# Splitting the output scales of the last three chunks between POOL and VectorE in a fused attention and expert kernel

## The chip, the cores and the metric

The kernel runs on one core of a Trainium2 chip. The metric is the time of one execution on the device in microseconds (us), the median of several runs. A profiled execution gives the trace from which the rows below are taken; its span is the time from the first to the last instruction that the profile shows.

## The reference

The input `x` is 2 x 512 tokens of 256 features, all in float32. It is normalised over its features to `xn`, and two blocks read `xn`; the result is `x + attention(xn) + experts(xn)`.

- Attention has 16 heads of 16 features: `q`, `k`, `v` and a gate from four 256x256 weights, scores `q k^T` times a decay `gamma^(i-j)` for j <= i (no softmax), `y = scores v`. Then `y` is normalised over its 256 features, `(y - mean) * rsqrt(var + 1e-5) * ln_w + ln_b`, multiplied by `silu(xn wg^T)` and projected by `wo`.
- The expert block routes each token to 4 of 32 experts (softmax over the 4 best router values, times 1.8). An expert is `silu(x gate^T) * (x up^T)` with 192 hidden features, then a projection back to 256. A shared expert of the same shape is added for every token.

The change concerns the factor `rsqrt(var + eps)` of the normalisation of `y`, here called the output scale, and `-mean * rsqrt(var + eps)`, here called the shift.

## The kernel before

The 1024 tokens are cut in 8 chunks of 128, numbered 0 to 7 and called turns where the loop over them is meant (the constant NT is 8, the constant CPB, chunks in a sequence, is 4). Each engine runs its own instructions in the order in which they were written; nothing is reordered, and the engines meet at semaphores only. An instruction that waits holds up all that is behind it on its engine.

The attention runs as one loop over the chunks, with the stages of neighbouring chunks interleaved by hand. In parallel the tokens are routed, and lists (codes) of the tokens of each expert are made. Then come the expert steps 0 to 16. A step handles a pair of experts, its units 2s and 2s+1 being the two experts: TensorE transposes gathered token rows, multiplies them by the gate and up weights (line 1575), ScalarE applies silu (lines 640, 641), VectorE multiplies (lines 1160, 1162), TensorE projects down (lines 1589, 1591), VectorE copies the result (line 1168) and POOL scatters it. The tail of the attention, that is the outputs of chunks 5, 6 and 7, is woven into expert steps 0 to 2. At the end come the shared expert and the weighted sum of the scattered rows.

The output of chunk t goes round the engines in this way:

1. TensorE ends `y` of the chunk (line 1515), ScalarE copies it (line 613), TensorE transposes it (line 1524), ScalarE copies it again (line 617, `ytok`).
2. VectorE takes mean and variance (`output_moments`, lines 1150 to 1153), and signals `mo_sb`.
3. POOL computes the scale (`output_scale`): the power -0.5 of the variance (line 794), one Newton step in two instructions (lines 795, 796), and the shift (line 797), which signals `nm_sb`. Each waits for the one before.
4. ScalarE normalises the chunk with scale and shift (`normalise_output`, line 624).
5. `gate_output` multiplies by `ln_w`, adds `ln_b` and multiplies by the gate. For chunks 2, 5, 6 and 7 that is done by VectorE (lines 1142, 1143, 1145), for the others by POOL (lines 806, 807, 809).
6. TensorE transposes it back (line 1532), ScalarE copies (line 609), TensorE projects (line 1541), VectorE adds the residual (line 1136, `res_sb`).

POOL also issues the gathers of token rows (line 830) and the scatters of results (line 838). Each of these is an indirect DMA; there are 36 of either, one for each block of 128 rows. The order on POOL from turn 6 on is: gathers 0 to 3, the decayed queries of chunk 7, gathers 4 and 5, the spread values of chunk 7, the scale of chunk 5, gather 6, the scale of chunk 6, gather 7, the scale of chunk 7, gathers 8 to 11, and then gathers and scatters in turn. TensorE's transposes of gathered rows (line 1553) take gathers 0 and 1 for the first pair, 2 and 3 for the second, 4 and 5 for the third.

The order on VectorE at the end of turn 7 is: the decayed scores of chunk 7, the moments of chunk 6. Then comes expert step 0: the multiplications of unit 0, gating of chunk 5, moments of chunk 7, gating of chunk 6, residual of chunk 5, multiplications of unit 1. In expert step 1: multiplications of unit 2, gating of chunk 7, multiplications of unit 3, residual of chunk 6.

The order on ScalarE there is: silu of unit 0, normalise chunk 5, copy the outputs of chunk 7 (line 613), the tokens of pair 1 (line 630), the output tokens of chunk 7 (line 617), silu of unit 1, the transposed chunk 5 (line 609), normalise chunk 6, the tokens of pair 2, silu of unit 2, the transposed chunk 6, normalise chunk 7.

The order on TensorE there is: transpose of chunk 7's outputs, gate and up of unit 1, transpose back of chunk 5; then expert step 1: transpose the rows of pair 2 (gathers 4 and 5), project chunk 5, gate and up of unit 2, transpose back of chunk 6, gate and up of unit 3, project chunk 6, down of pair 0, transpose back of chunk 7.

Two waits of TensorE belong to this stretch. The transpose back of a chunk writes the half bank from which the residual of the chunk before is read, and the gate and up matmuls of unit n write the bank of unit n - 2:

```python
need(pe, res_sb, t)            # transpose_back(t)
need(pe, h_sb, 2 * (n - 1))    # gate_up(n)
```

Functions and signals beyond these keep their meaning in the change. The functions that it touches, and those that call them:

Of the kernel before, what the change touches and what calls it, by code (L numbers as in the profile page):

```python
# [11 lines left out]
ALU = mybir.AluOpType  # L12
# [6 lines left out]
NT = TOK // P  # L19
# [31 lines left out]
YRING = 4  # L51
T_RANK, T_INVERT, T_EXPERT = 2, 6, 6
POOL_HOT = range(5, 10)
HOT_STEPS = {(3, "y"): 5, (4, "z"): 6, (4, "rows"): 2, (5, "tok"): 1, (5, "qk"): 2, (5, "vg"): 11}
HOT_PARTS = 2

# [89 lines left out]
def build(nc, x, consts, decay, w_router, w_qkvg, w_out, lnwb, rbias, w_exp, w_late, w_ovf2, w_shared, xn_rows, xnt_rows, y_rows, out):  # L146
    with ExitStack() as ctx:
# [3 lines left out]
        def sem(name):  # L151
            return ctx.enter_context(nc.semaphore(name))
# [9 lines left out]
        def early(*shape, dt=F32):  # L162

            n = int(np.prod(shape)) * mybir.dt.size(dt) // 4
            ap = arena[:, used[0]:used[0] + n]
            used[0] += n
            assert used[0] <= arena.shape[1]
            if dt != F32:
                ap = ap.bitcast(dt)
            if len(shape) == 2:  # L170
                ap = ap.rearrange("p (a b) -> p a b", a=shape[0])
            return ap
# [76 lines left out]
        ystats = early(6)  # L249
        yhalf = early(2)  # L250
        ynewton = early(1)
        yvar = early(2)
        minus_half = early(NT)
        ymv = early(2, 2)
        yrstd = early(2)
        shift_y = early(2)
# [81 lines left out]
        ytok_sb = sem("ytok_sb")  # L338
        mo_sb = sem("mo_sb")
        nm_sb = sem("nm_sb")  # L340
        vg_ps = sem("vg_ps")
        vg_sb = sem("vg_sb")
        xnt_out = sem("xnt_out")
# [432 lines left out]
        def _(pool):  # L776
            steps = [0]

            def step(ins):

                steps[0] += 1
                ins.then_inc(pool_seq, 1)
                pool.wait_ge(pool_seq, steps[0])
# [6 lines left out]
            def output_scale(t):  # L790

                s = slice(t % 2, t % 2 + 1)
                pool.wait_ge(mo_sb, t + 1)
                step(nc.gpsimd.tensor_tensor(yrstd[:, s], yvar[:, s], minus_half[:, 0:1], ALU.pow))
                step(nc.gpsimd.tensor_scalar(ynewton[:, :], yrstd[:, s], yrstd[:, s], yhalf[:, s], ALU.mult, ALU.mult))
                step(nc.gpsimd.tensor_scalar(yrstd[:, s], ynewton[:, :], 1.5, yrstd[:, s], ALU.add, ALU.mult))
                nc.gpsimd.tensor_scalar(shift_y[:, s], yrstd[:, s], ymv[:, t % 2, 0:1], -1.0, ALU.mult, ALU.mult
                                        ).then_inc(nm_sb, 1)
# [119 lines left out]
        def _(dve):  # L918
            steps = [0]

            def step(ins):

                steps[0] += 1
                ins.then_inc(dve_step, 1)
                dve.wait_ge(dve_step, steps[0])
# [131 lines left out]
            def one_hot_positions(part):  # L1057
                a = slice(part * NA // HOT_PARTS, (part + 1) * NA // HOT_PARTS)
                dve.wait_ge(abs_sb, a.stop - len(POOL_HOT))
                dve.wait_ge(pool_hot_sb, len(POOL_HOT))  # L1060
                nc.vector.tensor_scalar(pos_hot[:, a, :], pos_hot[:, a, :], 0.0, None, ALU.is_equal).then_inc(pos_hot_sb, 1)
# [72 lines left out]
            def add_residual(t):  # L1134
                dve.wait_ge(o_ps, t + 1)
                nc.vector.tensor_tensor(x_sb[:, t, :], x_sb[:, t, :], ps_po[:, D:2 * D], ALU.add).then_inc(res_sb, 1)

            def gate_output(t):
                dve.wait_ge(yn_sb, t + 1)
                if t in (CPB - 2, NT - 3):  # L1140
                    dve.wait_ge(z_sb, t)
                step(nc.vector.tensor_tensor(z1[:, :], yn[:, t % 2, :], lnw[:, :], ALU.mult))
                step(nc.vector.tensor_tensor(z1[:, :], z1[:, :], lnb[:, :], ALU.add))
                dve.wait_ge(vg_sb, 2 * (t + 1))
                nc.vector.tensor_tensor(z[:, t % 2, :], z1[:, :], gate[:, t % 3, :], ALU.mult).then_inc(z_sb, 1)

            def output_moments(t):
# [4 lines left out]
                nc.vector.tensor_scalar(yvar[:, t % 2:t % 2 + 1], ymv[:, t % 2, 1:2], EPS, None, ALU.add)  # L1152
                nc.vector.tensor_scalar(yhalf[:, t % 2:t % 2 + 1], ymv[:, t % 2, 1:2], EPS, -0.5, ALU.add, ALU.mult).then_inc(mo_sb, 1)

            def multiply_unit(n):

                dve.wait_ge(sil_sb, 2 * (n + 1))
                gu, p, c = ps_gu[n % 2], n // 2, slice(2 * P, 3 * P)
                need(dve, dn_ps, 2 * (p - 1))
                nc.vector.tensor_tensor(hA[:, n % 4, :], silA[:, n % 2, :], gu[:, P:2 * P], ALU.mult).then_inc(h_sb, 1)  # L1160
                half = slice(0, I2) if n % 2 == 0 else slice(I2, P)
                nc.vector.tensor_tensor(hC[half, p % 2, :], silC[0:I2, n % 2, :], gu[0:I2, c], ALU.mult).then_inc(h_sb, 1)
# [21 lines left out]
            def expert_step(s):  # L1184
                if s < PAIRS:
                    multiply_unit(2 * s)
                if s == 0:
                    gate_output(NT - 3)
                    output_moments(NT - 1)
                    gate_output(NT - 2)  # L1190
                    add_residual(NT - 3)
                if s == 1:
                    gate_output(NT - 1)
                if s == 2:
                    add_residual(NT - 1)
                    nc.vector.memset(o_mem.rearrange("p (j n) -> p j n", j=SUBS)[0:I2, :, XW:OW], 0.0).then_inc(oz_sb, 1)
                if s == PAIRS - 1:
                    results(s - 1)
                if s < PAIRS:
                    multiply_unit(2 * s + 1)  # L1200
                if s == 1:
                    add_residual(NT - 2)
                if s - 2 in O_BASE:
                    overflow_result(O_BASE.index(s - 2))
                if s - 1 in O_BASE:
                    dve.wait_ge(osil_sb, 2 * (O_BASE.index(s - 1) + 1))
                    multiply_overflow(oh_sb)
                if 1 <= s and s != PAIRS - 1:
                    results(s - 1)

            for t in range(NT):
                for r in range(HG // 2):
                    if t == NT - 1 and r == 2:
                        update_state(t - 1)
                    if t == T_INVERT and r == 3:
                        take_inverse()
                        make_codes()
                        find_block_experts()
                    decay_scores(t, r)
                    if t == 0 and r == 0:  # L1220
                        refine(2, slice(2, NT))
                        for u in range(2, 6):
                            normalise(u)
                if t == 0:
                    normalise(6)
                    normalise(7)
                if t == T_RANK - 1:
                    take_logits()
                if t % CPB > 0 and t < NT - 1:
                    update_state(t - 1)  # L1230
                if t == 0:
                    decay_keys(t)
                if t == T_RANK - 1:
                    choose_experts()
                if t == T_RANK:
                    mark_choices()
                if t == T_RANK + 1:
                    choose_slots()
                    assign_slots()
                if t == T_RANK + 2:  # L1240
                    gate_output(CPB - 2)
                    dve.wait_ge(pos_sb, 1)
                    one_hot_blocks()
                    add_residual(t - 2)
                if t >= 1:
                    output_moments(t - 1)
                if t == T_RANK - 1:
                    choices_as_numbers()
                if t == T_RANK:
                    take_ranks()  # L1250
                    count_blocks()
                if t == T_RANK + 3:
                    code_blocks(1)
                    one_hot_positions(0)
                if t == T_EXPERT:
                    weigh_choices()
                if 2 <= t < NT - 1 and t != T_RANK + 2:
                    add_residual(t - 2)
                if t == T_RANK:
                    shift_ranks()  # L1260
                if 0 < t % CPB < CPB - 1 or t == CPB:
                    decay_keys(t)
                if t == T_RANK + 2:
                    code_blocks(0)
                if t == T_RANK - 1:
                    spread_choices()
                if t == T_RANK + 3:
                    one_hot_positions(1)

            for s in range(PAIRS + 1):  # L1270
                expert_step(s)
# [630 lines left out]
```

## Time and profile before

| what | value |
|---|---|
| median of 3 runs | 200.17 us (200.09 to 200.4) |
| the profiled execution's own time | 200.26 us |
| its span | 198.4 us |
| TensorE's granted clock | full in every slice |
| turn 7 and expert step 0 on VectorE | about 76 to 87 us |

An engine's busy time is the sum of the times of its instructions. The chain of waits goes back from the last instruction to what released it, again and again, so that its pieces fill the span. In the timelines a row is an instruction or several alike ones; the bracket at its end says how long the engine was idle in front of it and which instruction of which engine, by line, released it. PEld is TensorE's loading of weights, which goes ahead of a matmul. Names such as `w_mem` cover many small tiles, so the line says what an instruction is.

### The profile page before, as it was taken

What the parts mean: (1) busy time and instruction counts of PE and PEld (TensorE: products, weight loads), DVE (VectorE), ACT (ScalarE), POOL (GpSimd) and SP (SyncE); (2) the same over time, 40 slices, a digit from 0 to 9 for tenths busy, and PEclk for the clock granted to TensorE, in tenths of its full rate; (3) what the DMA queues carried; (4) which work ended last, traced back from release to release, by engine and by line L of the source; (5) the groups of instructions that cost most, each with busy time, mean ns of one, the idle gap of its engine ahead of it and who ended that gap; (6) DMA issues with size and microseconds to landing.
All of it is one profiled execution on the core that took longest, in us unless ns stands there. A gap on an engine that the chain in (4) does not pass through costs nothing.

```text
span 198.4 us, 4872 instructions
## 1 busy us (share of the span) xinstructions
PE 190.0 (96%) x1734; PEld 142.7 (72%) x1734; DVE 117.5 (59%) x360; ACT 96.7 (49%) x242; POOL 111.8 (56%) x156
## 2 busy tenths in 40 slices
PE   8998999999998899899999999999999999999994
PEld 2665756778565667698888678887867877687863
DVE  3478789898897766765632532433342144426894
ACT  3146248555889342653238647734934941123500
POOL 4133057525979468777777677777877743730000
PEclk9999999999999999999999999999999999999999
DMA  4994999998000029999975634324433335229963
GB/s 133 316 374 159 332 403 421 446 444 378 7 0 3 5 56 380 384 358 366 366 288 149 223 106 140 97 90 138 123 104 98 115 91 220 79 82 292 373 262 132
DMA packets 15000, 42.33 MB, mean 213 GB/s; under 512 B 2677, under 2 KB 6138, under 8 KB 14336
## 3 DMA queue, kind: packets, MB, share of 16 engines
q1 hardware_dynamic: 11376, 33.03, 45.5%
q0 software_dynamic: 3456, 8.92, 13.3%
q8 instruction: 14, 0.23, 0.5%
q10 hardware_dynamic: 144, 0.07, 0.2%
q14 instruction: 10, 0.08, 0.1%
HBM read 34.66 MB, written 7.86 MB: 214 GB/s over the span
## 4 chain that ended last, share of the span: by engine, by line
PE 73%; DMA 7%; DVE 7%; issue 4%; POOL 4%; ACT 3%; SPq 0%; ACTq 0%; POOLq 0%; DVEq 0%
PE bank L1575 20%; PE bank L1591 8%; PE bank L1783 5%; PE bank L1589 5%; DMA xg_mem<-xn_rows,codes 4%; PE bank L1440 4%; PE bank L1450 3%; PE bank L1553 3%; DMA w_mem<-w_qkvg_dram 3%; PE bank L1541 3%; PE bank L1612 3%; PE bank L1515 3%; DVE w_mem L1105 2%; PE bank L1465 2%; PE bank L1817 2%
## 5 line engine op out<-in xcount | busy, mean ns | idle before, releaser
L1575 PE MATMUL bank<-xb_mem,w_mem 128*128 128x128 f32 x384 | 47.7, 276 | 0.1
L1575 PEld LDWEIGHTS bank<-xb_mem,w_mem 128*128 128x128 f32 x384 | 45.4, 192 | 0.8 <-issue 0.3
L838 POOL DMA_INDIRECT y_rows<-y_mem,codes x36 | 36.2, 1007 | 16.8 <-issue 9.4
L830 POOL DMA_INDIRECT xg_mem<-xn_rows,codes x36 | 35.4, 984 | 13.0 <-issue 9.7
L1160 DVE TENSOR_TENSOR h_mem<-h_mem,bank 128x128 f32<-128x128 f32 x32 | 9.2, 287 | 42.2 <-ACT h_mem L641 41.9
L1105 DVE TENSOR_TENSOR w_mem<-bank,w_mem 128x512 f32<-128x512 f32 x32 | 20.1, 682 | 2.9 <-PE bank L1465 2.8
L640 ACT ACTIVATE h_mem<-bank 128x128 f32<-128x128 f32 x32 | 8.9, 277 | 23.5 <-PE bank L1575 23.1
L1168 DVE COPY y_mem<-bank 128x256 f32<-128x256 f32 x36 | 15.0, 424 | 7.3 <-PE bank L1591 4.5
L653 ACT COPY w_mem<-w_mem 128x1024 f32 x16 | 16.0, 1042 | 3.2 <-PE bank L1630 2.2
L1591 PE MATMUL bank<-w_mem,h_mem 128*128 128x256 f32 x60 | 17.0, 405 | 0.0
L1440 PE MATMUL bank<-w_mem 128*128 128x128 f32 x128 | 15.9, 278 | 0.2 <-DMA w_mem<-w_qkvg_dram 0.2
L1440 PEld LDWEIGHTS bank<-w_mem 128*128 128x128 f32 x128 | 14.9, 192 | 1.1 <-ACT w_mem L566 0.7
L630 ACT COPY xb_mem<-bank 128x512 f32<-128x512 f32 x16 | 9.4, 585 | 12.6 <-PE bank L1553 12.4
L1450 PE MATMUL bank<-w_mem 128*128 128x512 f32 x32 | 15.1, 593 | 0.0
L1591 PEld LDWEIGHTS bank<-w_mem,h_mem 128*128 128x128 f32 x60 | 10.2, 189 | 5.8 <-issue 5.0
L574 ACT ACTIVATE w_mem<-bank,cst 128x256 f32<-128x256 f32 x16 | 6.7, 470 | 10.0 <-PE bank L1440 10.0
L1783 PE MATMUL bank<-xg_mem,ws_mem 128*128 128x256 f32 x48 | 11.0, 381 | 0.0
L1589 PE MATMUL bank<-w_mem,h_mem 64*128 64x256 f32 x60 | 10.5, 428 | 0.0
L1553 PE MATMUL bank<-cst,xg_mem 128*128 128x128 f32 x64 | 9.7, 275 | 0.7 <-DMA xg_mem<-xn_rows,codes 0.7
L1783 PEld LDWEIGHTS bank<-xg_mem,ws_mem 128*128 128x128 f32 x48 | 9.0, 190 | 1.5 <-DVE h_mem L1292 0.3
L787 POOL TENSOR_TENSOR w_mem<-w_mem,cst 128x256 f32<-128x256 f32 x6 | 5.3, 881 | 8.5 <-ACT w_mem L576 8.5
L1553 PEld LDWEIGHTS bank<-cst,xg_mem 128*128 128x128 f32 x64 | 7.7, 141 | 2.6 <-DMA xg_mem<-xn_rows,codes 0.9
(168 smaller groups left out, 320.7 us busy)
## 6 DMA issues: line engine op xcount, KB each, us to landing
w_mem<-w_exp_dram SPq DMA_DIRECT2D x3, 3456.0 KB, 21.6
w_mem<-w_late_dram SPq DMA_DIRECT2D x7, 1152.0 KB, 8.1
w_mem<-y_rows SPq DMA_DIRECT2D x8, 512.0 KB, 7.3
w_mem<-w_qkvg_dram SPq DMA_DIRECT2D x2, 512.0 KB, 6.3
w_mem<-decay_dram SPq DMA_DIRECT2D x2, 512.0 KB, 7.6
xn_rows<-w_mem SPq DMA_DIRECT2D x2, 512.0 KB, 3.4
xnt_rows<-w_mem SPq DMA_DIRECT2D x1, 1024.0 KB, 4.9
w_mem<-w_ovf_dram SPq DMA_DIRECT2D x16, 64.0 KB
```

The source lines that it names most:

```text
L653: return nc.scalar.copy(o_mem[:, j * OW:j * OW + XW], w_mem[:, bass.ds(e * EW, XW)])
L830: nc.gpsimd.indirect_dma_start(xg[:, k % RING, :], None, xn_rows, bass.IndirectOffsetOnAxis(ap=codes[:, c, 0:1], axis=0),).then_inc(tok_in ...
L838: nc.gpsimd.indirect_dma_start(y_rows, bass.IndirectOffsetOnAxis(ap=codes[:, c, 1:2], axis=0), ysb[:, k % YRING, :], None, bounds_check=RO ...
L1105: nc.vector.tensor_tensor(st[:, 4 * r * P:4 * (r + 1) * P], ps_s[r][:, :], dec[:, 4 * r * P:4 * (r + 1) * P], ALU.mult).then_inc(sc_sb, 1)
L1168: nc.vector.tensor_copy(ysb[:, w, :], ps[:, 0:D]).then_inc(ys_sb, 1)
L1440: last = nc.tensor.matmul(ps_qk[:, m * P:(m + 1) * P], wqkvg[:, g, m * P:(m + 1) * P], tokens(g, t), start=(g == 0), stop=(g == KT - 1))
L1450: last = nc.tensor.matmul(ps_vg[:, :], tokens(g, t), wqkvg[:, g, 2 * D:4 * D], start=(g == 0), stop=(g == KT - 1))
L1553: last = nc.tensor.transpose(ps_xt[p % 2][:, (2 * g + j) * P:(2 * g + j + 1) * P], xg[:, k % RING, g * P:(g + 1) * P], ident)
L1575: last = nc.tensor.matmul(ps_gu[j][:, m * P:(m + 1) * P], w[:, o:o + P], xbT[:, p % 2, (2 * g + j) * P:(2 * g + j + 1) * P], start=(g == 0 ...
L1589: nc.tensor.matmul(ps_dn[j][:, 0:D], hC[rows, p % 2, :], w2[rows], start=True, stop=False)
L1591: nc.tensor.matmul(ps_dn[j][:, 0:D], hA[:, 2 * (p % 2) + j, :], w[:, j * EW + KT * MB:j * EW + XW], start=False, stop=True).then_inc(dn_ps, 1)
L1783: last = nc.tensor.matmul(to, ws_mem[:, o:o + P], xnT_back[:, g, n], start=(g == 0), stop=(g == KT - 1))
```

## The change

For chunks 5, 6 and 7 POOL computes only the power (line 794) and signals it with a new semaphore, `root_sb`. The Newton step and the shift are done by VectorE, in a new function `finish_scale`, with the same operands; the shift there signals `nm_sb`. VectorE calls it for chunk 5 at the end of turn 7, behind the moments of chunk 6. In expert step 0 it calls it for chunk 6 behind the multiplications of unit 0, and for chunk 7 behind the gating of chunk 6. Chunks 0 to 4 stay as they are. The new `step` on VectorE is the same as the one there: the instruction signals, and VectorE waits for it before the next.

```diff
--- before.py
+++ after.py
@@ -51,6 +51,7 @@
 YRING = 4
 T_RANK, T_INVERT, T_EXPERT = 2, 6, 6
 POOL_HOT = range(5, 10)
+DVE_SCALES = (5, 6, 7)
 HOT_STEPS = {(3, "y"): 5, (4, "z"): 6, (4, "rows"): 2, (5, "tok"): 1, (5, "qk"): 2, (5, "vg"): 11}
 HOT_PARTS = 2
 
@@ -249,6 +250,7 @@
         ystats = early(6)
         yhalf = early(2)
         ynewton = early(1)
+        vnewton = early(1)
         yvar = early(2)
         minus_half = early(NT)
         ymv = early(2, 2)
@@ -338,6 +340,7 @@
         ytok_sb = sem("ytok_sb")
         mo_sb = sem("mo_sb")
         nm_sb = sem("nm_sb")
+        root_sb = sem("root_sb")
         vg_ps = sem("vg_ps")
         vg_sb = sem("vg_sb")
         xnt_out = sem("xnt_out")
@@ -791,6 +794,9 @@
 
                 s = slice(t % 2, t % 2 + 1)
                 pool.wait_ge(mo_sb, t + 1)
+                if t in DVE_SCALES:
+                    nc.gpsimd.tensor_tensor(yrstd[:, s], yvar[:, s], minus_half[:, 0:1], ALU.pow).then_inc(root_sb, 1)
+                    return
                 step(nc.gpsimd.tensor_tensor(yrstd[:, s], yvar[:, s], minus_half[:, 0:1], ALU.pow))
                 step(nc.gpsimd.tensor_scalar(ynewton[:, :], yrstd[:, s], yrstd[:, s], yhalf[:, s], ALU.mult, ALU.mult))
                 step(nc.gpsimd.tensor_scalar(yrstd[:, s], ynewton[:, :], 1.5, yrstd[:, s], ALU.add, ALU.mult))
@@ -1152,6 +1158,15 @@
                 nc.vector.tensor_scalar(yvar[:, t % 2:t % 2 + 1], ymv[:, t % 2, 1:2], EPS, None, ALU.add)
                 nc.vector.tensor_scalar(yhalf[:, t % 2:t % 2 + 1], ymv[:, t % 2, 1:2], EPS, -0.5, ALU.add, ALU.mult).then_inc(mo_sb, 1)
 
+            def finish_scale(t):
+
+                c = slice(t % 2, t % 2 + 1)
+                dve.wait_ge(root_sb, t - DVE_SCALES[0] + 1)
+                step(nc.vector.tensor_scalar(vnewton[:, :], yrstd[:, c], yrstd[:, c], yhalf[:, c], ALU.mult, ALU.mult))
+                step(nc.vector.tensor_scalar(yrstd[:, c], vnewton[:, :], 1.5, yrstd[:, c], ALU.add, ALU.mult))
+                nc.vector.tensor_scalar(shift_y[:, c], yrstd[:, c], ymv[:, t % 2, 0:1], -1.0, ALU.mult, ALU.mult
+                                        ).then_inc(nm_sb, 1)
+
             def multiply_unit(n):
 
                 dve.wait_ge(sil_sb, 2 * (n + 1))
@@ -1185,9 +1200,11 @@
                 if s < PAIRS:
                     multiply_unit(2 * s)
                 if s == 0:
+                    finish_scale(NT - 2)
                     gate_output(NT - 3)
                     output_moments(NT - 1)
                     gate_output(NT - 2)
+                    finish_scale(NT - 1)
                     add_residual(NT - 3)
                 if s == 1:
                     gate_output(NT - 1)
@@ -1266,6 +1283,8 @@
                     spread_choices()
                 if t == T_RANK + 3:
                     one_hot_positions(1)
+                if t == NT - 1:
+                    finish_scale(NT - 3)
 
             for s in range(PAIRS + 1):
                 expert_step(s)
```

## Rows read from the trace of the kernel before

**Rows 1.** The page, part 1: busy us of each engine, share of the span, instructions

```profile
PE 190.0 (96%) x1734; PEld 142.7 (72%) x1734; DVE 117.5 (59%) x360; ACT 96.7 (49%) x242; POOL 111.8 (56%) x156
```

**Rows 2.** The chain of waits, expert step 1: start us, us, what

```profile
87.46 1.52 PE bank L1575 x12
```

**Rows 3.** TensorE's waits, 75 to 198 us: us in total, times, longest

```profile
PE bank L1553 <- DMA xg_mem<-xn_rows,codes: 0.7, 1, 0.7
PE bank L1804 <- DVE h_mem L1295: 0.3, 1, 0.3
PE bank L1603 <- DVE h_mem L1162: 0.2, 1, 0.2
PE bank L1524 <- ACT w_mem L613: 0.2, 1, 0.2
```

**Rows 4.** Timeline of VectorE, turn 7 and step 0: start us, us, line, [idle before]

```profile
80.37 0.14 DVE L1153 TENSOR_SCALAR w_mem<-w_mem 128x1 f32<-128x1 f32 x1
80.43 0.28 DVE L1160 TENSOR_TENSOR h_mem<-h_mem,bank 128x128 f32<-128x128 f32 x1
...
81.31 0.42 DVE L1142 TENSOR_TENSOR w_mem<-w_mem 128x256 f32<-128x256 f32 x1 [0.42 <-ACT w_mem L624]
...
85.05 0.42 DVE L1142 TENSOR_TENSOR w_mem<-w_mem 128x256 f32<-128x256 f32 x1 [1.54 <-ACT w_mem L624]
...
86.00 0.43 DVE L1145 TENSOR_TENSOR w_mem<-w_mem 128x256 f32<-128x256 f32 x1
86.34 0.41 DVE L1136 TENSOR_TENSOR x_sb<-x_sb,bank 128x256 f32<-128x256 f32 x1
...
86.98 0.28 DVE L1162 TENSOR_TENSOR h_mem<-h_mem,bank 64x128 f32<-64x128 f32 x1
```

**Rows 5.** Timeline of POOL, scales of chunks 5 to 7 and gathers

```profile
78.89 0.58 POOL L794 TENSOR_TENSOR w_mem<-w_mem 128x1 f32<-128x1 f32 x1
...
80.39 0.26 POOL L797 TENSOR_SCALAR w_mem<-w_mem 128x1 f32<-128x1 f32 x1
81.09 1.06 POOL L830 DMA_INDIRECT xg_mem<-xn_rows,codes  x1 [0.44 <-issue]
...
87.81 1.05 POOL L830 DMA_INDIRECT xg_mem<-xn_rows,codes  x1 [0.44 <-issue]
```

**Rows 6.** Timeline of ScalarE in the same stretch

```profile
80.68 0.60 ACT L624 ACTIVATE w_mem<-w_mem 128x256 f32<-128x256 f32 x1 [0.74 <-POOL w_mem L797]
81.30 0.37 ACT L613 COPY w_mem<-bank 128x256 f32<-128x256 f32 x1
...
83.84 0.27 ACT L641 ACTIVATE h_mem<-bank 64x128 f32<-64x128 f32 x1
...
84.41 0.60 ACT L624 ACTIVATE w_mem<-w_mem 128x256 f32<-128x256 f32 x1
```

**Rows 7.** Timeline of TensorE's weight loads in the same stretch

```profile
81.73 0.20 PEld L1524 LDWEIGHTS bank<-cst,w_mem 128*128 128x128 f32 x2 [0.46 <-ACT w_mem L613]
...
83.23 0.25 PEld L1532 LDWEIGHTS bank<-cst,w_mem 128*128 128x128 f32 x2
84.38 0.42 PEld L1553 LDWEIGHTS bank<-cst,xg_mem 128*128 128x128 f32 x4 [0.89 <-DMA xg_mem<-xn_rows,codes]
...
86.97 0.25 PEld L1532 LDWEIGHTS bank<-cst,w_mem 128*128 128x128 f32 x2
87.38 1.42 PEld L1575 LDWEIGHTS bank<-xb_mem,w_mem 128*128 128x128 f32 x12 [0.16 <-issue]
```

**Rows 8.** Timeline of VectorE: short instructions that wait for one another

```profile
5.13 0.16 DVE L932 TENSOR_TENSOR w_mem<-w_mem 128x1 f32<-128x1 f32 x1
5.33 0.16 DVE L933 SCALAR_TENSOR_TENSOR w_mem<-w_mem 128x1 f32<-128x1 f32 x1
...
68.29 0.25 DVE L1082 TENSOR_SCALAR w_mem<-w_mem,cst 128x60 f32<-128x60 f32 x1
68.58 0.22 DVE L1084 SCALAR_TENSOR_TENSOR w_mem<-w_mem 128x60 f32<-128x60 f32 x1
```

## The prediction

> **What bounds the kernel now.** I read the page's busy shares first [rows 1]: TensorE is busy for 96% of the span, VectorE for 59%, POOL for 56%. So work taken from POOL is worth something only where TensorE waits for it, directly or through others. The chain of waits comes second: from 84.41 us to the end of the expert steps it is TensorE's own matmuls, piece touching piece, and the gate/up matmuls of unit 3, the place that will matter, are one of the pieces [rows 2]. A delay there is a delay of the end, unless a later wait takes it up. Third, whom TensorE waits for after 75 us: 0.7 us once for gathered rows, and 0.2 to 0.3 us three times for ScalarE or VectorE [rows 3]. Then I read the place of the change engine by engine, in the timelines of VectorE, POOL, ScalarE and TensorE's weight loads, which show when TensorE may go on [rows 4 to 7].
>
> What the reader should see there is a ring of in-order engines. VectorE ends the moments of chunk 6 at 80.51 (80.37 + 0.14); the next instruction, which does not wait for them, starts at 80.43, 0.06 behind the start of their last [rows 4]. POOL has long computed the power of chunk 5 (78.89 to 79.47) and delivers its shift at 80.65 [rows 5]. ScalarE, idle for 0.74 us for just that, normalises chunk 5 at 80.68, and only then copies chunk 7's outputs at 81.30 [rows 6]; TensorE's transpose of these waits 0.46 us for the copy and loads at 81.73 [rows 7]. So the scale of chunk 5 is already on TensorE's path, through ScalarE's order.
>
> **The change, part by part.** *POOL.* For each of chunks 5, 6 and 7 three instructions go; for chunk 5 the stretch from the end of the power to the end of the shift is 80.65 − 79.47 = 1.18 us [rows 5]. Behind it stand gather 6, the power of chunk 6, gather 7, the power of chunk 7, gathers 8 and on. Gather 6 starts 0.44 us behind the scale as now, at 79.91 instead of 81.09, and the power of chunk 6 ends at about 79.91 + 1.06 + 0.58 = 81.55. The power of chunk 7 must wait for that chunk's moments, which VectorE now ends at 85.05 − 1.54 = 83.51 [rows 4] and will end 0.76 us later (below), at 84.27; with 0.06 for the signal and 0.58 for itself it is done at 84.9, and gather 8 starts at about 85.4 instead of 87.81 [rows 5]. POOL gains 2.4 us on the gathers from 8 on. It is worth nothing to TensorE: its one wait for gathered rows, at 84.38 [rows 7], is for gathers 4 and 5, and both are issued before chunk 5's scale in POOL's order.
>
> *One finish on VectorE.* Three 128x1 instructions, each waiting for the one before. No row shows a 128x1 with two scalars from memory. The nearest is the refinement at the start, also 128x1 and each waiting for the one before: starts 0.20 us apart, 0.16 us long [rows 8]. The upper bound is a 128x60 with one scalar from memory, 0.25 us long and 0.29 from its start to that of the instruction that waits for it [rows 8]; the lower is a 128x1 that is 0.14 long and holds up the next, which does not wait for it, by 0.06 [rows 4]. I take 0.20. Then the shift is there 2 × 0.20 + 0.16 = 0.56 us after the start, and whatever stands behind is put off by 2 × 0.20 + 0.06 = 0.46 us (bounds 0.18 and 0.64).
>
> The Trainium skill has a lower price (VectorE: DVE Perf Modes, section The TRN2 errata — SBUF-src ops pay a fixed extra latency per instruction): 58 cycles plus the row length at 0.96 GHz for an instruction from SBUF to SBUF, from which I estimate 0.06 us for each of the three. The page itself says that its row is too low for one instruction alone, and the refinement's 0.16 us bear that out [rows 8]; by the rule the sum below would come down to about 0.2 us.
>
> *Chunk 5.* Its finish stands behind chunk 6's moments, so it starts at 80.43, though the power has been there since 79.47. The shift comes at 80.99, and ScalarE starts 0.03 later, as now, at 81.02 instead of 80.68: +0.34 us. Everything behind it on ScalarE is tied to it: the copy of chunk 7's outputs 81.30 → 81.64, TensorE's transpose 81.73 → 82.07 and the gate/up of unit 1 behind it, the gate of unit 1 (83.84 → 84.18), the normalising of chunk 6 (84.41 → 84.75) [rows 6, 7]. TensorE itself gets the 0.34 us back, since at 84.38 it has stood idle for 0.89 us for the gathers [rows 7]; ScalarE does not. If the gathers landed earlier this cover would go, at 0.34 us, but the delay below is longer and takes it in.
>
> *Chunk 6.* Its finish stands behind unit 0's multiplications, which end 0.46 us later than now, and waits for the power at 81.55, so it runs from about 81.61; VectorE's gating of chunk 5 starts at 82.07 instead of 81.31, +0.76 [rows 4]. This third of the change is hidden: a gating takes 86.00 + 0.43 − 85.05 = 1.38 us [rows 4], so chunk 5's ends at 83.45, and TensorE's transpose back of chunk 5 wants it at 83.23 + 0.34 = 83.57 [rows 7]. Were it later, the idle time in front of 84.38 would pay. The shift of chunk 6, at 82.2, is not awaited: ScalarE reaches chunk 6 at 84.75.
>
> *Chunk 7, where it costs.* VectorE's gating of chunk 6 follows ScalarE, 85.05 → 85.39 [rows 4]. Behind it now stands chunk 7's finish (its power is there at 84.9), 0.46 us, and behind that the residual of chunk 5 and the multiplications of unit 1. Both are 0.34 + 0.46 = 0.80 us late. Two waits of TensorE hang on them. The transpose back of chunk 6 needs the residual of chunk 5, since both use one bank: 86.34 + 0.41 + 0.80 = 87.55, plus 0.06 for the signal (as from ScalarE's end at 81.67 to the load at 81.73 [rows 6, 7]), 87.61 instead of 86.97: 0.64 us. The gate/up matmuls of unit 3 need unit 1 multiplied, since they write its bank: 86.98 + 0.28 + 0.80 + 0.06 = 88.12 instead of 87.38 [rows 4, 7]. Together TensorE is 88.12 − 87.38 = 0.74 us late; in the trace of before the same chain leaves it 0.06 us to spare. Chunk 7's shift comes at 87.3, ahead of ScalarE's need of it.
>
> *Behind that.* ScalarE and VectorE follow TensorE, and of its waits there none is for something that keeps its own time: two rows remain, both for VectorE's multiplications that follow TensorE's own matmuls [rows 3]. So nothing gives the 0.74 us back. Sum: 0.34 + 0.46 − 0.06 = 0.74 us. With the lower price the shift comes at 80.43 + 0.12 + 0.14 = 80.69, +0.04, and the sum is 0.04 + 0.18 − 0.06 = 0.16; with the upper at 80.43 + 0.58 + 0.25 = 81.26, +0.61, and it is 0.61 + 0.64 − 0.06 = 1.19. The profiled execution took 200.26 us, 1.86 of it outside the span; 201.00 it would be. It lies 0.09 above the median of the runs, 200.17, so I forecast 200.91 us, with 200.33 and 201.36 for the bounds.
>
> **The rivals.** *Cheap finishes.* The small instructions run at the pace of those that do not wait, 0.06 us [rows 4]: 200.33 us, no change that can be told. For it: most of a short instruction's time is overlapped on this engine. Against: each of the three waits for the last, as in the refinement [rows 8]. *POOL's lead pays.* Gathers 6 to 11 are issued 1.2 to 2.4 us earlier; if that shortened what TensorE waits for, and the finishes fell into VectorE's idle time, the wait of 0.7 us [rows 3] would be the gain: about 199.5 us, faster. It decides from the point at which gathers 4 and 5 land before TensorE is there (84.38 − 0.89 = 83.49). For it: VectorE stands idle 1.54 us ahead of chunk 6's gating [rows 4]. Against: gathers 4 and 5 are ahead of the removed work, and chunk 7's finish stands behind that idle time, not in it. *More than the sum.* Scalars from memory cost more than any row shows, or the power of chunk 6 comes so late that chunk 5's gating holds TensorE beyond the gathers: from 201.4 us to about 201.7 (a finish of 0.8 us in both terms). *Not doing what it says:* chunk 7's power waits for moments that are themselves later, so POOL's lead may be smaller than 2.4 us; as nobody waits for it, the time would be the forecast's, and it has no chance of its own.
>
> **How the numbers follow.** A measurement of this kernel can tell about 0.2%, 0.4 us, from no change. The forecast's own band, 200.6 to 201.4 us, gets 0.65; cheap finishes, or a delay partly taken up, 200.0 to 200.6, get 0.17; POOL's lead 0.08; more than the sum 0.10. The band and the last are slower by over 0.2%, 0.75; the second is no change, the third faster. The range, 200.3 to 201.5, takes in both bounds and leaves out POOL's lead, part of the second case and most of the worst.
>
> **What would show it.** Right: ScalarE's wait ahead of chunk 5's normalising grows from 0.74 to about 1.1 us and is for VectorE; the finish's instructions start about 0.20 us apart; TensorE's transpose back of chunk 6 and its gate/up of unit 3 wait for VectorE, together 0.74 us; the stretch from there to the end is as long as before; gather 8 starts near 85.4. Wrong: unit 3 starting less than 0.3 us later than 87.38; a later wait of TensorE that has become shorter; or scalars from memory that do not keep the refinement's pace.

## Result and the profile after

The changed kernel takes 203.69 us (median of 6 runs, 203.01 to 204.39), the kernel before, run beside it, 200.25 us: the ratio is 1.0161, 95% interval 1.0129 to 1.0192. It is slower, as forecast, but by 3.4 us and not by 0.7, and outside the range.

The profiled execution after took 203.01 us, span 201.2 us. Line numbers are 3 to 19 higher than before. TensorE's waits after 75 us, and the timelines of VectorE, ScalarE, TensorE's weight loads and POOL follow, in the order of [rows 3], [rows 4], [rows 6], [rows 7] and [rows 5]; their columns are the same.

```profile
PE bank L1543 <- ACT w_mem L616: 0.8, 1, 0.8
PE bank L1551 <- DVE x_sb L1142: 0.5, 1, 0.5
...
PE bank L1560 <- ACT w_mem L612: 0.3, 1, 0.3
```

```profile
81.82 0.14 DVE L1159 TENSOR_SCALAR w_mem<-w_mem 128x1 f32<-128x1 f32 x1
81.88 0.27 DVE L1165 TENSOR_SCALAR w_mem<-w_mem 128x1 f32<-128x1 f32 x1
82.18 0.21 DVE L1166 TENSOR_SCALAR w_mem<-w_mem 128x1 f32<-128x1 f32 x1
82.43 0.21 DVE L1167 TENSOR_SCALAR w_mem<-w_mem 128x1 f32<-128x1 f32 x1
82.56 0.28 DVE L1175 TENSOR_TENSOR h_mem<-h_mem,bank 128x128 f32<-128x128 f32 x1
...
83.63 0.41 DVE L1148 TENSOR_TENSOR w_mem<-w_mem 128x256 f32<-128x256 f32 x1
...
88.31 0.27 DVE L1165 TENSOR_SCALAR w_mem<-w_mem 128x1 f32<-128x1 f32 x1
...
88.99 0.41 DVE L1142 TENSOR_TENSOR x_sb<-x_sb,bank 128x256 f32<-128x256 f32 x1
...
89.62 0.28 DVE L1177 TENSOR_TENSOR h_mem<-h_mem,bank 64x128 f32<-64x128 f32 x1
```

```profile
82.68 0.60 ACT L627 ACTIVATE w_mem<-w_mem 128x256 f32<-128x256 f32 x1 [1.28 <-DVE w_mem L1167]
```

```profile
83.72 0.20 PEld L1543 LDWEIGHTS bank<-cst,w_mem 128*128 128x128 f32 x2 [1.00 <-ACT w_mem L616]
...
85.59 0.42 PEld L1572 LDWEIGHTS bank<-cst,xg_mem 128*128 128x128 f32 x4
86.56 0.73 PEld L1560 LDWEIGHTS bank<-w_mem 128*128 128x128 f32 x4 [0.56 <-ACT w_mem L612]
...
90.02 1.08 PEld L1594 LDWEIGHTS bank<-xb_mem,w_mem 128*128 128x128 f32 x9 [0.31 <-issue]
```

```profile
80.34 0.57 POOL L798 TENSOR_TENSOR w_mem<-w_mem 128x1 f32<-128x1 f32 x1
...
85.86 0.56 POOL L798 TENSOR_TENSOR w_mem<-w_mem 128x1 f32<-128x1 f32 x1 [1.96 <-DVE w_mem L1159]
86.59 1.00 POOL L836 DMA_INDIRECT xg_mem<-xn_rows,codes  x1 [0.18 <-issue]
```

The gate and up matmuls of unit 3 load at 90.02 us instead of 87.38 [rows 7]: 2.64 us late. Behind them next to nothing is lost: from there to the end of the span it is 201.2 − 90.0 = 111.2 us, before 198.4 − 87.4 = 111.0. The reader should now ask how much of the 2.64 us was there before the first moved instruction ran, and compare an instruction that the change doesn't touch: the last instruction of chunk 6's moments, which ends a run without waits, starts at 81.82 instead of 80.37 [rows 4], 1.45 us late. VectorE is already 1.46 us late at 76.88 us, where the same instruction started at 75.42 before. So only 2.64 − 1.46 = 1.18 us arise where the prediction looked.

The 1.46 us come together earlier: 0.21 us before 58.5 us, the rest at 60 us. These are the rows of before there, POOL's, VectorE's, and TensorE's wait:

```profile
58.51 0.64 POOL L806 TENSOR_TENSOR w_mem<-w_mem 128x256 f32<-128x256 f32 x1 [0.25 <-ACT w_mem L624]
59.22 0.64 POOL L807 TENSOR_TENSOR w_mem<-w_mem 128x256 f32<-128x256 f32 x1
59.94 0.64 POOL L809 TENSOR_TENSOR w_mem<-w_mem 128x256 f32<-128x256 f32 x1
```

```profile
60.09 1.50 DVE L1070 TENSOR_TENSOR h_mem<-xb_mem,cst 128x960 bf16<-128x960 bf16 x1
```

```profile
PE bank L1532 <- POOL w_mem L809: 0.8, 1, 0.8
```

And the same after:

```profile
58.72 0.73 POOL L812 TENSOR_TENSOR w_mem<-w_mem 128x256 f32<-128x256 f32 x1 [0.25 <-ACT w_mem L627]
59.53 0.72 POOL L813 TENSOR_TENSOR w_mem<-w_mem 128x256 f32<-128x256 f32 x1
60.33 1.69 POOL L815 TENSOR_TENSOR w_mem<-w_mem 128x256 f32<-128x256 f32 x1
```

```profile
60.30 1.15 DVE L1076 TENSOR_TENSOR h_mem<-xb_mem,cst 128x960 bf16<-128x960 bf16 x1
```

```profile
PE bank L1551 <- POOL w_mem L815: 2.0, 1, 2.0
```

POOL's gating of chunk 3 is the same code on the same data, but each product takes 0.73 us instead of 0.64. So the third starts at 60.33, 0.03 behind VectorE's product of two inputs in SBUF, where before it started 0.15 ahead of that. Whichever of the two starts second is stretched: before VectorE's took 1.50 us instead of 1.15, after POOL's took 1.69 instead of 0.73. And POOL's is on the path: TensorE's transpose back of chunk 3 waits for it, 0.8 us before and 2.0 after.

The Trainium skill describes this (SBUF — State Buffer, section SBUF: two separate sides): VectorE and GpSimd share a pair of ports as an exclusive lock, also for a VectorE instruction with two SBUF inputs against a GpSimd instruction that reads SBUF, and the one that starts second is blocked. The rows above agree as to who is blocked: 60.30 + 1.15 = 61.45 us is when VectorE's ends, and POOL's ends 0.57 behind that. That is less than the 0.73 us which POOL's product takes alone; what it did ahead of the block no row shows.

### The profile page after: what moved, and what is told of

The parts are those of the page before. It is cut to its first block, busy times and chain, and to the rows that moved or that the text cites. A ratio compares the mean times of both kernels' runs of the same rounds, so it can differ in the third digit from the quotient of the medians.

```text
span 201.2 us, 4872 instructions
## 1 busy us (share of the span) xinstructions
PE 190.1 (95%) x1734; PEld 142.7 (71%) x1734; DVE 118.9 (59%) x369; ACT 96.8 (48%) x242; POOL 110.2 (55%) x147
## 4 chain that ended last, share of the span: by engine, by line
PE 75%; DVE 10%; ACT 4%; DMA 3%; POOL 3%; issue 2%; SPq 1%; ACTq 0%; POOLq 0%; DVEq 0%
PE bank L1594 20%; PE bank L1610 8%; PE bank L1802 5%; PE bank L1608 5%; PE bank L1469 4%; PE bank L1459 4%; DVE w_mem L1111 3%; DMA w_mem<-w_qkvg_dram 3%; PE bank L1534 3%; PE bank L1560 3%; PE bank L1631 3%; PE bank L1572 3%; PE bank L1484 3%; PE bank L1836 2%; ACT xg_mem L594 2%
## 5 line engine op out<-in xcount | busy, mean ns | idle before, releaser
L1334 DVE SCALAR_TENSOR_TENSOR x_sb<-w_mem,rw,x_sb 128x256 f32<-128x256 f32 x22 | 9.5, 477 | 0.2
L1534 PE MATMUL bank<-w_mem 128*32 128x128 f32 x256 | 8.7, 275 | 0.7 <-ACT w_mem L569 0.7
```

## Experiments

Theory A has two causes. First, the diff adds a one-word tile, `vnewton`, in front of some of the tiles that POOL's gating reads and writes (`yn`, `z1`, `z`); it moves these by 4 bytes, POOL's products get slower, and the third loses the race with VectorE. Second, the moved steps cost TensorE 1.18 us, a finish holding VectorE for 0.68 us. The chief rival, B, puts the whole loss on the moved steps. Each kernel ran beside the kernel before on its chip (median 200.53 us for the first group, 200.52 for the second, 200.37 for the third).

**The whole change, the tile laid behind all others** (first group):

```diff
-        vnewton = early(1)          # after ynewton
         zT = early(KT * P)
+        vnewton = early(1)
```

> The change as it is, but the one-word tile of the new Newton step is laid behind all the other tiles of its region, so that no other tile moves by a word. Theory A (the one word moves the tiles behind it; POOL's gating instructions then take 0.73 us instead of 0.64, and the third of chunk 3 starts just behind a VectorE instruction with two inputs in SBUF and is held by it for 1.06 us; the moved steps themselves cost 1.2 us): POOL's gating back at 0.64 us, TensorE's wait for POOL near 60 us back from 2.0 to 0.8, time about 201.4 us. Theory B (the moved steps alone make all of the 3.4 us, and what differs ahead of 76 us is chance): 203.4 to 203.9.

201.73 us, ratio 1.0058 (1.0040 to 1.0076). POOL's products take 0.64 us again and TensorE's wait at 60 us is 0.8. The waits after 75 us are those of the change, 0.8, 0.5 and 0.3, and unit 3 is 1.19 us late, counted from a stretch that begins 0.07 later. By the medians the moved steps are worth 1.20 us; B falls.

**The kernel before with one unused word at that place** (first group):

```diff
         ynewton = early(1)
+        unused_word = early(1)
```

> The kernel before with one unused word in the place where the change lays its new tile; nothing else. Theory A: POOL's gating at 0.73 us, TensorE's wait near 60 us 2.0 us long, time 200.25 + 1.3 to 2.2 = 201.5 to 202.4 (the upper end if TensorE's granted clock dips as in most runs of the change). Theory B: 200.2, as before.

202.61 us, 1.0104 (1.0075 to 1.0133), with every instruction as before. In the profile's groups of instructions (busy us, mean ns) POOL's three products, and TensorE's wait:

```profile
L810 POOL TENSOR_TENSOR w_mem<-w_mem 128x256 f32<-128x256 f32 x4 | 3.9, 971 | 0.3
L807 POOL TENSOR_TENSOR w_mem<-w_mem 128x256 f32<-128x256 f32 x4 | 3.2, 793 | 4.6 <-ACT w_mem L625 4.6
L808 POOL TENSOR_TENSOR w_mem<-w_mem 128x256 f32<-128x256 f32 x4 | 2.9, 728 | 0.3
```

```profile
PE bank L1533 <- POOL w_mem L810: 2.0, 1, 2.0
```

One word costs 2.08 us alone. With the 1.20 us of the moved steps that is 3.28, of the 3.44 measured; the rest is within the intervals.

**The change, with one useless 0.42-us instruction on VectorE ahead of its product** (first group):

```diff
+                nc.vector.bn_stats(...)      # result unused
                 code_blocks(1)
```

> The change as it is, with one more instruction on VectorE (a repeat of the moments' first, 0.42 us, one input) ahead of the 128x960 product that holds POOL near 60 us. Theory A: POOL's third gating instruction of chunk 3 starts first and runs its 0.73 us, VectorE's waits for it; TensorE's wait near 60 us falls to about 0.9 us, time 1.0 to 1.7 us below the change, 202.0 to 202.7, although VectorE has more to do. Rival C (POOL is slow there by itself, for its address or its code): no gain, 203.7 to 204.1.

202.00 us, 1.0068 (1.0054 to 1.0083): 1.5 us above before where the change is 3.4 above it, though VectorE does more. POOL and VectorE at 60 us:

```profile
60.61 0.72 POOL L815 TENSOR_TENSOR w_mem<-w_mem 128x256 f32<-128x256 f32 x1
```

```profile
61.02 1.33 DVE L1076 TENSOR_TENSOR h_mem<-xb_mem,cst 128x960 bf16<-128x960 bf16 x1
```

POOL's third product is first again and takes 0.72 us; the wait is 1.0. So the 0.09 us a product are cheap by themselves, and the order of the two starts is what costs. Rival C, a POOL that is slow there by itself, falls as the cause of the wait.

**Tile at the end, and chunk 7's finish behind the multiplications of unit 1** (first group):

```diff
                     gate_output(NT - 2)
-                    finish_scale(NT - 1)
 ...
                 multiply_unit(2 * s + 1)
+                if s == 0:
+                    finish_scale(NT - 1)
```

> As the first of these, and the finish of chunk 7 stands behind the multiplications of unit 1 instead of in front of the residual of chunk 5. Theory A: 0.6 to 0.7 us less than the first, since only the 0.54 us of chunk 5's shift are left: 200.7 us; TensorE's two waits in expert step 1 fall from 1.2 to 0.5 us. Theory B: no different from the first by more than 0.2 us.

201.31 us, 1.0041 (1.0025 to 1.0057). The wait at the transpose back of chunk 6 is gone, and unit 3 is 0.52 us late instead of 1.19. The trace shows the 0.67 us that were expected, the medians 0.42, and the time stays above the 200.7 expected, by more than the 0.28 that this chip is slower. What remains is chunk 5's finish: the waits for ScalarE (0.8 and 0.4), and with it chunk 6's gating, which VectorE starts at 85.78 instead of 85.05 us in a stretch that begins 0.18 later.

**Chunk 5 back on POOL, chunk 6's finish as in the change, chunk 7's late** (second group; tile at the end, `DVE_SCALES = (6, 7)`):

> The new tile behind all others, chunk 5's scale whole on POOL as before, chunk 6's finish on VectorE where the change has it, chunk 7's behind the multiplications of unit 1. Theory A (of the moved steps only the 0.54 us of chunk 5's later shift and the 0.68 us of chunk 7's finish ahead of unit 1 reach TensorE, and both are gone here; POOL's lead is worth nothing): within 0.3 us of before on the same chip, 0.3 to 0.7 us below the run with chunk 7 late and chunk 5 moved. Rival D (anything moved to VectorE there costs, the third finish too): 0.4 us or more above before.

A miss: 201.79 us, 1.0068 (1.0052 to 1.0084), 1.27 us above before. The number is in rival D's range, but the rows give another reason than a price for anything moved. VectorE, then POOL, then TensorE's wait:

```profile
82.54 0.27 DVE L1165 TENSOR_SCALAR w_mem<-w_mem 128x1 f32<-128x1 f32 x1 [1.91 <-POOL w_mem L798]
...
83.22 0.41 DVE L1148 TENSOR_TENSOR w_mem<-w_mem 128x256 f32<-128x256 f32 x1
```

```profile
81.92 0.58 POOL L798 TENSOR_TENSOR w_mem<-w_mem 128x1 f32<-128x1 f32 x1
```

```profile
PE bank L1550 <- DVE w_mem L1151: 1.4, 1, 1.4
```

With chunk 5's small steps back on POOL, the power of chunk 6 comes at 82.50, and VectorE stands in front of it for 1.91 us with the gating of chunk 5 queued behind. Chunk 6's finish is free in the change only because chunk 5's steps have left POOL. That I had not seen.

**Chunk 5's finish ahead of the moments of chunk 6, chunk 6's behind the gating of chunk 5, chunk 7's late; gathers 4 and 5 ahead of the decayed queries** (second group; tile at the end; of the diff the places of the first two finishes):

```diff
+                if t == NT - 1:
+                    finish_scale(NT - 3)
                 output_moments(...)          # of chunk 6
 ...
-                    finish_scale(NT - 2)
                     gate_output(NT - 3)
+                    finish_scale(NT - 2)
```

> The three finishes on VectorE in other places, and gathers 4 and 5 ahead of the decayed queries of chunk 7 on POOL: chunk 5's finish ahead of chunk 6's moments, chunk 6's behind the gating of chunk 5, chunk 7's behind the multiplications of unit 1; new tile behind all others. Theory A (ScalarE's start on chunk 5 sets TensorE's pace through step 0, with the gathers next in line): the shift of chunk 5 at about 80.4 instead of 80.65, gathers 0.9 us earlier, TensorE at unit 3 about 0.3 to 0.4 us earlier than before: 0.1 to 0.5 us below before on the same chip. Rival D: no faster than before, 0 to 0.8 us above it.

A second miss: 200.74 us, 1.0017 (0.9995 to 1.0038), no difference from before that can be told, where 0.1 to 0.5 us less was expected. ScalarE still waits as long as before:

```profile
80.85 0.60 ACT L627 ACTIVATE w_mem<-w_mem 128x256 f32<-128x256 f32 x1 [0.73 <-DVE w_mem L1168]
```

In this order the finishes cost nothing that can be told, and they gain nothing: chunk 5's shift ends at 80.82 us, not at the 80.4 expected. One reason is in VectorE's rows: its state update, of two SBUF inputs, now runs beside POOL's decayed queries and takes 0.83 us for two instead of 0.58.

**Two and five unused words in the kernel before** (second group):

> The kernel before with two unused words in the place of the new tile. If POOL's time depends on whether the moved tiles lie an odd or an even number of words from the two others that it reads, its gating is back at 0.64 us and the time at before's; if on any other rule of the address (any shift costs), 0.73 us and 1 to 2 us above before.

> The kernel before with five unused words there, so that the moved tiles lie a whole number of 128 bytes from the start of the region. If even words cost, 0.73 us for POOL's gating, TensorE's wait near 60 us 2.0 us, 1 to 2 us above before; if alignment to a larger unit helps, 0.64 us or less and no loss.

202.49 us, 1.0100 (1.0080 to 1.0120), and 201.78 us, 1.0077 (1.0048 to 1.0107). In both POOL's first two products take 0.72 to 0.73 us, the third is blocked, and TensorE waits 2.0. So it isn't a matter of odd and even words.

**Sixteen, eight and four unused words** (third group; four words apart, with one run of each kernel):

> The kernel before with 16 unused words (64 bytes) where the change has its one-word tile; no instruction differs. If the time of POOL's 128x256 products depends on where the tiles lie within a line of 64 bytes: 0.64 us as before, TensorE's wait for POOL at 60 us stays 0.8 us, time as before within 0.3 us. If it depends on anything wider, or on the distance to the tiles that did not move: 0.73 us, the wait 2.0 us, and 1.2 to 2.2 us more.

> The kernel before with 8 unused words (32 bytes) there. If the place within 32 bytes decides: 0.64 us and the time of before within 0.3 us. If the place within 64 bytes decides, and not that within 32: 0.73 us and 1.2 to 2.2 us more, while 16 words cost nothing.

> The kernel before with 4 unused words (16 bytes) in the same place. If POOL's 128x256 products keep their time when the tiles move by 16 bytes: 0.64 us and a wait of TensorE of 0.8 us at 60 us. If only moves by whole multiples of 32 bytes are free: 0.73 us, the wait 2.0 us, and the time 1.2 us or more above the kernel before.

200.57 us, 1.0003 (0.9985 to 1.0021); 200.53 us, 1.0005 (0.9989 to 1.0021); and 200.36 us beside 200.59 for the kernel before. The three products and the wait with four words:

```profile
L810 POOL TENSOR_TENSOR w_mem<-w_mem 128x256 f32<-128x256 f32 x4 | 2.5, 636 | 0.3
L807 POOL TENSOR_TENSOR w_mem<-w_mem 128x256 f32<-128x256 f32 x4 | 2.5, 635 | 3.4 <-ACT w_mem L625 3.4
L808 POOL TENSOR_TENSOR w_mem<-w_mem 128x256 f32<-128x256 f32 x4 | 2.5, 633 | 0.3
```

```profile
PE bank L1533 <- POOL w_mem L810: 0.8, 1, 0.8
```

Moves of 16, 32 and 64 bytes cost nothing, moves of 4, 8 and 20 bytes do: the place within 16 bytes decides; a move of 12 bytes wasn't tried. The Trainium skill names 16 bytes as the line of this memory, each crossing to a new line having its price (SBUF — State Buffer, section Specifications (TRN2)); the unit of the runs agrees with it, but that crossings are the cause isn't shown.

Whether it is the place itself or that in relation to the operands that did not move (`lnw`, `lnb`, the gate) no experiment tells apart, but the allocation in the kernel's text says more. Counted from the start of their region, `lnw`, `lnb` and the gate lie at multiples of 16 bytes. The moved tiles lie 12 bytes past one in the fast kernel before, and at a multiple of 16 in the slow ones with one and five words. So 16-byte alignment is not what makes the product fast. And the decayed queries, a POOL product of the same shape whose first operand and result also lie 12 bytes past a multiple of 16 in that region, take 0.73 us in the kernel before:

```profile
75.25 0.73 POOL L787 TENSOR_TENSOR w_mem<-w_mem,cst 128x256 f32<-128x256 f32 x1
```

The place of these two alone therefore doesn't decide; that of the second operand, here in `cst`, has a part.

**Only chunk 7's finish on VectorE: where the change has it, and behind the multiplications of unit 1** (third group; tile at the end, `DVE_SCALES = (7,)`):

> Chunks 5 and 6 are scaled whole on POOL as before; only chunk 7's finish (two Newton instructions and the shift) is on VectorE, in the place that the change gives it, between the gating of chunk 6 and the residual of chunk 5. The new tile lies behind zT. Theory A (a finish holds VectorE for 0.68 us, as in the trace after, and TensorE's waits at the transpose back of chunk 6 and at unit 3 pass it on, less 0.06 to spare): unit 3's gate/up about 0.6 us later than before, time 0.5 to 0.7 us above the kernel before. Theory F (by the prediction's 0.46 us a finish): 0.3 to 0.4 us above. Rival D (the power without the other instructions on POOL disturbs something else): not within either.

> As the one before, but chunk 7's finish stands behind the multiplications of unit 1, where no wait of TensorE hangs on it. Theory A: the same time as the kernel before within 0.2 us; POOL's two instructions less and its shift less for chunk 7 are worth nothing. Rival (POOL's lead is worth something once VectorE's order costs nothing): 0.3 us or more below the kernel before.

201.05 us, 1.0038 (1.0024 to 1.0051), and 200.67 us, 1.0017 (1.0003 to 1.0032). TensorE's weight loads for unit 3, first in place, then late:

```profile
87.76 1.42 PEld L1591 LDWEIGHTS bank<-xb_mem,w_mem 128*128 128x128 f32 x12 [0.31 <-issue]
```

```profile
87.32 1.41 PEld L1592 LDWEIGHTS bank<-xb_mem,w_mem 128*128 128x128 f32 x12 [0.31 <-issue]
```

Against chunk 6's gating, which starts at 84.75 and 84.99 us (85.05 before), that is 0.68 us late in the first and on time in the second. So one finish in front of the residual costs its full 0.68 us, by the time 0.7, and theory F with 0.46 a finish is out. The late one costs nothing at unit 3; its median lies 0.3 us above before, more than the 0.2 expected. Where that is the traces don't show, and it stays open; the kernel above with all three finishes on VectorE and chunk 7's late is likewise 0.26 us slower by its median (0.78) than by its trace (0.52). In neither is POOL's lead worth anything.

## Why the prediction was wrong

**The step that failed first: the sum begins at 80.43 us.** The part-by-part account takes every row ahead of the first moved instruction as unchanged, and prices what the diff removes, adds and moves among instructions only. The new tile is not in it at all. In the trace it cost 1.46 us at the start of the stretch, and in most runs more (last section); that it is the tile's doing is shown by the kernels with the tile at the end and with the unused word. No rival covers it: *more than the sum* looked at scalars and at the power of chunk 6. In the profile of before there was a sign to be read: POOL's gating stood on the path, 0.15 us from a collision with VectorE.

**The second, a mis-sized term: a finish taken at 0.20 us an instruction.** Its three instructions start 0.30 and 0.25 us apart and last 0.27, 0.21 and 0.21 us: the shift is there 0.76 us after the start (0.56 forecast), and what stands behind is held 0.68 us (0.46). The refinement reads no scalar from memory; here the first instruction reads two (0.27 us), the others one each (0.21). The nearest row in pace was the 128x60 [rows 8], which has one and was taken as the upper bound. With the bound the sum was 1.19 us, and the trace shows 2.64 − 1.46 = 1.18. That the two agree is partly luck, for the terms differ: chunk 5's is 0.54 at its start and 0.51 by the end of chunk 6's gating instead of 0.61, the finish 0.68 instead of 0.64. And the 0.06 to spare isn't there: from the end of unit 1's multiplications to the load for unit 3 it is 0.12 us before (87.26 to 87.38, [rows 4, 7]) and after (89.90 to 90.02), so this wait was at its limit already, and the 0.06 for the signal, taken from ScalarE, was too short for it. The estimate of 0.06 us from the Trainium skill (VectorE: DVE Perf Modes, section The TRN2 errata) is contradicted by the 0.21.

**What was right.** *Chunk 5:* ScalarE's wait is for VectorE and grows from 0.74 to 1.28 us [rows 6], at the forecast place, 0.54 instead of 0.34. *The gathers:* the 0.89 us ahead of pair 2 [rows 7] are gone: TensorE loads these rows 1.21 us later than before and no longer waits for them, while ScalarE gets nothing back. (The cover was a little larger than forecast: the rows landed at least 0.24 us sooner after their issue than in the trace of before, which nothing in the change explains.) One link I missed: projecting chunk 5 now waits 0.3 us for ScalarE's copy; it adds nothing, since unit 3 is held for longer by VectorE. *Chunk 6:* hidden, with the gating of chunk 5 at 83.63 − 1.46 = 82.17 (82.07 forecast); the cover is POOL's lead, as the miss with chunk 5 back on POOL showed. *Chunk 7:* the transpose back of chunk 6 waits 0.5 us for the residual, and unit 3 follows the multiplications; the kernels with only chunk 7 confirm place and price. *POOL's lead:* gather 8 at 86.59 − 1.46 = 85.13 (85.4 forecast, with 0.44 us from the scale to the gather; behind the power alone it is 0.18), POOL idle for 1.96 us ahead of the last power, and nothing gained. *Behind:* the rest is as long as before within 0.2 us.

## What to carry to other kernels

A diff that adds a tile moves every tile behind it: price that as a part of the change, put small new tiles last or fill them up to 16 bytes, so that the others keep their places within 16 bytes, and compare durations of untouched instructions before looking at the touched ones. Where two engines that block each other start 0.15 us apart on the path, a small shift can turn the order (here 0.18 us, two products of 0.09 more each), and the price is close to the length of the instruction that now goes first (here 0.96 us, 1.69 instead of 0.73, behind one of 1.15). A short serial computation handed to another engine costs its full pace, with its own operand forms, in front of whatever is queued behind it; place it behind the work that others wait for.

## What the runs showed of the hardware

*POOL and addresses.* A 128x256 float32 product on POOL takes 0.635 us or 0.73 us by where its tiles lie within 16 bytes, in the kernels with moves of 0, 4, 8, 16, 20, 32 and 64 bytes.

*The clock after an idle time.* In five of the six runs of the changed kernel the granted clock averages 0.992 over the span, in the one profiled here 1.0. The profile with one unused word caught where: windows of 1 us, busy share of PE, PEld, DVE, ACT and POOL (with instructions), then the granted clock.

```profile
60.00:61.00 1.00, 0.01 (x1) 0.00 (x0) 0.97 (x4) 0.92 (x3) 0.92 (x2) 1.00 0.00 0
61.00:62.00 1.00, 0.00 (x0) 0.00 (x0) 1.00 (x2) 0.00 (x0) 1.00 (x2) 1.00 0.06 16
62.00:63.00 1.00, 0.98 (x18) 0.57 (x18) 0.51 (x1) 0.51 (x2) 1.00 (x1) 0.87 0.00 0
63.00:64.00 1.00, 1.00 (x6) 0.80 (x3) 0.00 (x0) 1.00 (x5) 0.90 (x3) 0.50 0.00 0
64.00:65.00 1.00, 1.00 (x3) 0.37 (x2) 0.00 (x0) 1.00 (x5) 0.80 (x5) 0.50 0.00 0
65.00:66.00 1.00, 1.00 (x21) 0.83 (x24) 0.42 (x1) 1.00 (x5) 0.25 (x2) 0.50 0.00 0
66.00:67.00 1.00, 1.00 (x25) 0.63 (x18) 0.00 (x0) 0.86 (x4) 0.00 (x0) 0.92 0.00 0
```

TensorE had done nothing for 2 us and was at work again from 62.02 us; the clock then fell to half, the 1.2 GHz level, and came back after 3 to 4 us. The price is read from TensorE's rows of this kernel (first) and of the one with five words, whose clock stayed full behind the same 2.0-us wait:

```profile
63.11 2.08 PE L1542 MATMUL bank<-w_mem 128*128 128x256 f32 x4
...
68.26 0.95 PE L1423 MATMUL bank<-h_mem,xg_mem 128*128 128x120 bf16 x15
```

```profile
62.94 1.13 PE L1542 MATMUL bank<-w_mem 128*128 128x256 f32 x4
...
67.47 1.74 PE L1423 MATMUL bank<-h_mem,xg_mem 128*128 128x120 bf16 x30 [0.93 <-DVE xg_mem L1062]
```

The matmuls take 2.08 us instead of 1.13, and 68.26 − 67.47 = 0.79 us are left behind the next wait. The medians agree: 2.08 us above before with one word, 1.26 with five. In the changed kernel and with one and five words every run with the fall is slower than every run without it; with two words the four runs don't separate. In the runs of these kernels an average of 0.992 or less stands in 4 of 6 with one word, 3 of 4 with two and 1 of 4 with five, and in none of the kernels where the wait at 60 us is 0.8 to 1.0 us. That the longer idle time brings the fall isn't shown: the two go together, without an experiment on the idle time alone; why it comes in some runs and not in others is open. Its 0.79 us are of the size of the gap between the 2.75 us of the profiled executions and the 3.44 us of the medians.
